# One store per batch of units in place of four, put ahead of a load; the second batch norm's turns moved up, with units and matmuls on zeros about them

## The chip, the cores and the metric

The kernel runs on one core of one Trainium2 chip, as one program with one launch. The metric is the device time in microseconds of that core, from one execution to the next; three runs of the kernel before are shown. One further execution was profiled, and all rows below are from it. TensorE is called PE, VectorE DVE, ScalarE ACT, GpSimd POOL and SyncE SP. SP does nothing here but issue DMA transfers, one after the other, each behind the waits that stand ahead of it.

## The reference

Four graph layers over 512 nodes with 512 features each are run one after the other; ahead of each stands a layer norm and a relu, and behind each a residual sum. Cut to what matters here:

```python
h = relu(layernorm(x)); x = x + L0(h)      # attention with an adjacency mask, feed-forward
h = relu(layernorm(x)); x = x + L1(h)      # linear + prelu, then two convolutions
#   for l in range(2):
#       h = prelu((x + agg(x)) @ conv_W1[l].T + b1[l]) @ conv_W2[l].T + b2[l]
#       h = (h - mean) * rsqrt(var + eps) * gamma[l] + beta[l]     # batch norm over the nodes
#       x = relu(h)
h = relu(layernorm(x)); x = x + L2(h)      # normalised aggregation, then a product with W
h = relu(layernorm(x)); x = x + L3(h)      # two gated relational layers
#   w[r] = sum over 30 bases b of att[r, b] * basis[b]             # 2 x 512 x 512 from 30 x 512 x 512
```

The weights `w` of the two relational layers of L3 depend on no activation. They are sums over 30 bases of 512 x 512 floats, so some 63 MB have to be read for the two layers.

## The kernel before, in words

Node features are kept as [128 partitions, 4 tiles, 512]. Products in float32 precision are made of three matmuls on rounded parts (`_hi`, `_lo`), 128 x 512 each. Every engine runs its own list of instructions in the order in which the code writes them; semaphores tie the lists together. Nothing is reordered.

**Units.** The sum over the bases is cut into 64 units (32 for each relational layer). Unit `u` needs one load of 128 partitions x 2048 floats (1 MB) from `in_basis` into `bring[:, u % 4]`, and four matmuls of 120 rows into 32 columns (`units`, L1241 to L1259), which add into one PSUM bank for each batch of four units. The units are written between the stages of the other layers, so PE has work while they wait for others. When the four units of batch `b` are done, ACT copies the bank into `stage[:, b % 3]` (`stage_units`, L453 to L463; 128 partitions x 512 floats), and SP stores that to `w_scratch` in DRAM. POOL later loads `w_scratch` of a layer as a whole.

**SP's order** (L300 to L319). For `n` from 0, SP issues the load of unit `n` once unit `n - 4` is done (`basis_used`). After the loads with `n % 4 == 3`, from `n = 11` on, it waits until batch `n // 4 - 2` is staged and issues its store, as four transfers of 32 partitions each, since the rows of the four column tiles `j` lie 32 units apart in `w_scratch`. So the load of unit `n + 1` stands behind the store.

**The end of the second batch norm** (PE, L1547 to L1569). PE does the second product of convolution 1 (`c2_1`), then `units(4)` (units 53 to 56), then turns the four normalised tiles `s1` back into node order with 16 transposes (L1554 to L1560), for which it waits tile by tile on `bn1`, then `units(3)` (57 to 59), then the first quarter of the aggregation of the next layer (`aggregate`, L1294 to L1318), unit 60, the other three quarters, unit 61, and the product `gcn`. On ACT the last two batch norm pieces (L605) are followed by the copy of batch 13 (L462), the root of the degrees (L656), and the roots, relus and casts of the layer norm (L419, L662, L665). DVE adds the turned tiles to `xr` (L1118), makes the statistics, and the low parts `x_lo` (L1132), of which the aggregation needs one more for each quarter.

**Matmuls on zeros.** `keep_clock(n)` (L1347 to L1350) does `n` matmuls on a tile of zeros into PSUM bank 7, 128 x 512 in bf16. Before, it is used only at the very beginning.

Of the kernel before, what the change touches and what calls it, by code (L numbers as in the profile page):

```python
# [28 lines left out]
P = 128  # L29
# [39 lines left out]
RELS = 2  # L69
KB = C * BASES  # L70
Q = RELS * C
COLT = 4
UNITS = P // COLT
BATCH = 4
BATCHES = UNITS // BATCH
SLOTS = 3
# [39 lines left out]
def build(nc, x, src, dst, etype, weights, rows, cols, alphas, att, basis, scratch, out):  # L116
    with ExitStack() as ctx:
# [5 lines left out]
        def sem(name):  # L123
            if name not in names:
                names[name] = ctx.enter_context(nc.semaphore(name))
            return names[name]

        bank = [ctx.enter_context(nc.psum_tensor(f"bank{i}", [P, N], F32)) for i in range(4)]
# [3 lines left out]
        def places(*uses):  # L132

            made = []
            for use in uses[:-1]:
# [20 lines left out]
        gate_rows = hT  # L156
# [14 lines left out]
        stage, attw, _, landing, y1_hi, y1_lo = places(  # L171
            [("stage", [P, SLOTS, D], F32), ("attw", [P, 2, BATCH, 32], F32),
             ("unused2", [P, D - 2 * BATCH * 32], F32), ("landing", [P, C, D], F32)],
            [("y1_hi", [P, C, D], F32R), ("y1_lo", [P, C, D], F32R)])
# [34 lines left out]
        zeros = sb("zeros", [P, N], BF16)  # L209
# [23 lines left out]

        def stored(slot, groups):

            return sum(b % SLOTS == slot for b in range(groups)) * COLT * 16

        def weight_parts(name):
            if PARTS[name][0] is None:
# [42 lines left out]
        with nc.Block() as block:  # L282

            @block.sync
            def _(sp):
# [7 lines left out]
                for layer in range(2):  # L293
                    for c in range(C):
                        for r in range(RELS):
                            q = r * C + c
                            sp.dma_start(attw[c * BASES:(c + 1) * BASES, layer, 0, q:q + 1],
                                         att[layer, r, :].rearrange("(b a) -> b a", a=1)).then_inc(
                                             sem("att_loaded"), 16)
                for n in range(2 * UNITS + 2 * BATCH):  # L300
                    if n < 2 * UNITS:
                        if n >= BATCH:
                            sp.wait_ge(sem("basis_used"), n - BATCH + 1)
                        rows = P if n + 1 < 2 * UNITS else KB
                        sp.dma_start(bring[0:rows, n % BATCH, :, :],
                                     basis_rows[n * KB:n * KB + rows, :, :]).then_inc(
                                         sem(f"basis{n % BATCH}_loaded"), 16)
                    if n % BATCH == BATCH - 1 and n >= 3 * BATCH - 1:

                        b = n // BATCH - 2  # L310
                        sp.wait_ge(sem("stage_ready"), b + 1)
                        layer, g = divmod(b, BATCHES)
                        if b == 2 * BATCHES - 1:
                            sp.wait_ge(sem("gate_rows"), 16 * 2 * RELS)
                        for j in range(COLT):
                            at = j * UNITS + g * BATCH
                            sp.dma_start(scratch[layer, at:at + BATCH, :, :].rearrange("g q o -> (g q) o"),
                                         stage[32 * j:32 * j + 32, b % SLOTS, :]).then_inc(
                                             sem(f"w_stored{b % SLOTS}"), 16)  # L319
                for c in range(C):  # L320
                    sp.wait_ge(sem("rel1_out_sum"), c + 1)
                    sp.dma_start(out[:, c, :], hr[:, c, :]).then_inc(sem("out_stored"), 16)
# [904 lines left out]
            def _(pe):  # L1227
# [116 lines left out]
                    mm.then_inc(sem("qkv"[which] + "_psum"), 1)  # L1344

                first, every = FIRST_TILE, TILE_EVERY
                def keep_clock(n):  # L1347

                    for _ in range(n):
                        pe.matmul(bank[7][:, :], zeros[:, 0:P], zeros[:, :], start=True, stop=True)  # L1350

                pe.wait_ge(sem("zeros"), 1)
                keep_clock(12)
# [4 lines left out]
                for n in range(ECH):  # L1358
# [3 lines left out]
                    t, at = divmod(n - first, every)  # L1362
# [128 lines left out]
                for c in range(C):  # L1491
                    for k in range(2 * C):
# [4 lines left out]
                        for i, j in ((0, 0), (0, 1), (1, 0)):  # L1497
                            mm = pe.matmul(bank[c][:, :], (ff1_hi, ff1_lo)[i][k // C][:, k % C, blk(P, c)],  # L1498
                                           weight_parts("f2a" if k < C else "f2b")[j][:, k % C, :],
                                           start=(k == 0 and i == j), stop=(k == 2 * C - 1 and i == 1))  # L1500
# [47 lines left out]
                parts_stage("c1_1", hT_parts, "agg1", "c1_1_psum")  # L1548
                units(1)
                parts_stage("c2_1", x_parts, "c1_1", "c2_1_psum")  # L1550
                units(4)

                pe.wait_ge(sem("c2_1"), C)
                for f in range(C):  # L1554

                    pe.wait_ge(sem("bn1"), f + 1)
                    for c in range(C):
                        mm = pe.transpose(bank[c][:, blk(P, f)], s1[:, f, blk(P, c)], ident[:, :])
                        if f == C - 1:
                            mm.then_inc(sem("x4_psum"), 1)  # L1560
                units(3)

                pe.wait_ge(sem("x5"), 2)
                aggregate("h_gcn_parts", "agg2_psum", order=ALL_BANKS[:C], banks=AGG2_BANKS)
# [132 lines left out]
```

## Time and profile before

| | |
|---|---|
| three runs of the kernel before | 463.43, 464.56, 468.84 us (median 464.56) |
| profiled execution, its own time | 463.99 us |
| its span, first to last instruction | 462.2 us |
| PE busy | 442.4 us (96% of the span) |
| DVE busy | 340.3 us (74%) |
| ACT busy | 241.0 us (52%) |
| POOL busy | 38.4 us (8%) |
| basis loads | 64, of which 63 of 1024 KB and one of 960 KB |
| stores of `stage` | 64 of 64 KB |
| bytes moved by DMA | 99.23 MB, 215 GB/s over the span |

The span is 1.8 us shorter than the execution's own time. A page or a view of the trace gives times in microseconds from the start of the span. Units show as `x8` for one unit, since a float32 matmul is recorded as two. The lines L1256, L1270 and so on are those of the kernel before; those behind L300 have moved by one in the changed kernel.

### The profile page before, as it was taken

What the parts mean: (1) busy time and instruction counts of PE and PEld (TensorE: products, weight loads), DVE (VectorE), ACT (ScalarE), POOL (GpSimd) and SP (SyncE); (2) the same over time, 40 slices, a digit from 0 to 9 for tenths busy, and PEclk for the clock granted to TensorE, in tenths of its full rate; (3) what the DMA queues carried; (4) which work ended last, traced back from release to release, by engine and by line L of the source; (5) the groups of instructions that cost most, each with busy time, mean ns of one, the idle gap of its engine ahead of it and who ended that gap; (6) DMA issues with size and microseconds to landing.
All of it is one profiled execution on the core that took longest, in us unless ns stands there. A gap on an engine that the chain in (4) does not pass through costs nothing.

```text
span 462.2 us, 6176 instructions
## 1 busy us (share of the span) xinstructions
PE 442.4 (96%) x2202; PEld 273.4 (59%) x2202; DVE 340.3 (74%) x725; ACT 241.0 (52%) x421; POOL 38.4 (8%) x59
## 2 busy tenths in 40 slices
PE   5999999899899999999999999999599999999996
PEld 3434434344343334878776866676267688888885
DVE  3897876899999969879779657675758785866212
ACT  3998784586798634663335436445542533511210
POOL 3330000012311200010010000100000000000000
PEclk8899999999999999999999999999889999999999
DMA  7997535123999999856099766772990740000002
GB/s 261 417 365 170 198 116 211 61 92 142 357 397 403 379 386 384 328 164 246 0 358 423 292 238 255 279 251 71 401 340 26 296 150 34 1 0 2 0 3 91
DMA packets 18906, 99.23 MB, mean 215 GB/s; under 512 B 3903, under 2 KB 4287, under 8 KB 8383
## 3 DMA queue, kind: packets, MB, share of 16 engines
q1 hardware_dynamic: 14151, 72.86, 42.2%
q0 software_dynamic: 4000, 25.18, 14.8%
q10 hardware_dynamic: 720, 0.73, 0.5%
q8 instruction: 22, 0.36, 0.3%
q14 instruction: 13, 0.11, 0.1%
HBM read 93.50 MB, written 5.25 MB: 214 GB/s over the span
## 4 chain that ended last, share of the span: by engine, by line
PE 82%; DMA 10%; DVE 6%; issue 1%; ACT 1%; DVEq 0%; SPq 0%; ACTq 0%
PE bank L1270 18%; PE sbank L1592 9%; DMA bring<-in_basis 9%; PE sbank L1256 8%; PE bank L1343 7%; PE sbank L1326 6%; PE bank L1605 6%; PE bank L1498 5%; PE bank L1577 5%; PE bank L1256 3%; PE bank L1310 3%; PE sbank L1236 3%; PE sbank L1310 3%; PE sbank L1381 2%; PE bank L1404 2%; PE sbank L1458 2%
## 5 line engine op out<-in xcount | busy, mean ns | idle before, releaser
L1256 PE MATMUL sbank<-bring,attw 120*32 120x512 f32 x320 | 40.3, 612 | 4.9 <-DMA bring<-in_basis 4.9
L762 DVE TENSOR_SCALAR cnt<-iota_row,edge_f 128x512 bf16<-128x512 f16 x132 | 40.8, 345 | 4.4 <-PE sbank L1326 4.4
L509 ACT ACTIVATE adjT<-distance,edge_w,edge_f 128x128 bf16<-128x128 bf16 x61 | 29.2, 480 | 2.0 <-PE sbank L1326 2.0
L1326 PE MATMUL sbank<-cnt,adjT 128*128 128x512 bf16 x132 | 30.0, 380 | 0.0
L419 ACT ACTIVATE stat<-stat,eps 128x1 f32<-128x1 f32 x32 | 9.4, 295 | 39.0 <-DVE stat L772 39.0
L1343 PE MATMUL bank<-hT,wring 128*128 128x512 f32 x64 | 28.9, 594 | 0.0
L1185 DVE SCALAR_TENSOR_TENSOR y_lo<-sbank,gate,y_hi 128x512 fp32r<-128x512 f32 x16 | 11.8, 749 | 22.6 <-ACT y_hi L690 22.6
L448 ACT ACTIVATE s<-bank,colsb 128x512 f32<-128x512 f32 x24 | 16.4, 687 | 21.8 <-PE bank L1270 21.8
L1256 PE MATMUL bank<-bring,attw 120*32 120x512 f32 x192 | 23.7, 600 | 2.6 <-DMA bring<-in_basis 2.5
L759 DVE TENSOR_SCALAR adjT<-iota_row,edge_f,edge_w 128x128 bf16<-128x128 f16 x71 | 22.1, 311 | 5.4 <-PE sbank L1326 5.4
L480 ACT ACTIVATE distance<-iota_row,edge_f 128x128 bf16<-128x128 f16 x61 | 24.3, 400 | 1.7
L1270 PE MATMUL bank<-hT_hi,w_hi 128*128 128x512 f32 x64 | 25.2, 393 | 0.0
L1270 PE MATMUL bank<-hT_hi,w_lo 128*128 128x512 f32 x64 | 25.0, 390 | 0.0
L1270 PE MATMUL bank<-hT_lo,w_hi 128*128 128x512 f32 x64 | 24.9, 389 | 0.0
L1592 PE MATMUL sbank<-w_hi,xT_hi 128*128 128x512 f32 x64 | 24.9, 389 | 0.0
L1592 PE MATMUL sbank<-w_lo,xT_hi 128*128 128x512 f32 x64 | 24.9, 389 | 0.0
L1592 PE MATMUL sbank<-w_hi,xT_lo 128*128 128x512 f32 x64 | 24.9, 389 | 0.0
L1326 PEld LDWEIGHTS sbank<-cnt,adjT 128*128 128x128 bf16 x132 | 12.3, 98 | 20.5 <-issue 3.6
L1256 PEld LDWEIGHTS sbank<-bring,attw 120*32 120x32 f32 x320 | 8.0, 110 | 26.2 <-issue 19.2
L690 ACT ACTIVATE y_hi<-sbank,gate 128x512 fp32r<-128x512 f32 x16 | 10.8, 688 | 23.8 <-PE sbank L1592 23.8
L531 ACT ACTIVATE s<-s 128x1024 f32<-128x1024 f32 x16 | 16.8, 1058 | 12.2 <-DVE s L947 11.7
L381 POOL TENSOR_TENSOR s<-s,row_sum 128x768 f32<-128x768 f32 x7 | 12.8, 1823 | 94.7 <-ACT row_sum L541 94.7
(227 smaller groups left out, 1062.8 us busy)
## 6 DMA issues: line engine op xcount, KB each, us to landing
bring<-in_basis SPq DMA_DIRECT2D x63, 1024.0 KB, 8.2
wring<-in_weights POOLq DMA_DIRECT2D x8, 1024.0 KB, 10.0
landing<-in_weights POOLq DMA_DIRECT2D x4, 1024.0 KB, 7.2
w_scratch<-stage SPq DMA_DIRECT2D x64, 64.0 KB, 8.0
hT<-in_weights POOLq DMA_DIRECT2D x4, 1024.0 KB, 10.4
qkw<-w_scratch POOLq DMA_DIRECT2D x2, 2048.0 KB, 8.1
rring<-in_rows POOLq DMA_DIRECT2D x12, 256.0 KB, 8.6
hT<-w_scratch POOLq DMA_DIRECT2D x4, 256.0 KB, 6.9
```

The lines of the kernel that those rows point to most:

```text
L480: act.activation(distance[:, i % 2, :], iota[:, 0:P], ACT.Abs, scale=-1.0, bias=dst_lo[:, n:n + 1]).then_inc(sem("distance"), 1)
L509: act.activation(hot_d[:, n % HOT, :], distance[:, i % 2, :], ACT.Relu, scale=minus_w[:, n:n + 1], bias=weight_f[:, n:n + 1]).then_inc(sem ...
L762: dve.tensor_scalar(hot_s[:, n % HOT, :], iota[:, :], src_f[:, n:n + 1], None, ALU.is_equal).then_inc(sem("hot_ready"), 1)
L1256: mm = pe.matmul(unit_bank(b)[32 * j:32 * j + 32, :], attw[0:KB, u // UNITS, g, :], bring[0:KB, u % BATCH, j, :], start=(g == 0), stop=(g ...
L1270: mm = pe.matmul(bank[c][:, :], lhs[:, k, blk(P, c)], rhs[:, k, :], start=(k == 0 and i == j), stop=(k == C - 1 and i == 1))
L1310: mm = pe.matmul(bank[banks[c]][:, :], x[:, k, blk(P, c)].bitcast(dt), counts[:, k, :], start=(k == 0 and i == 0), stop=(k == C - 1 and i ...
L1326: pe.matmul(bank[7][:, :], hot_d[:, n % HOT, :], hot_s[:, n % HOT, :], start=(n == 0), stop=(n == ECH - 1)).then_inc(sem("hot_used"), 1)
L1343: mm = pe.matmul(bank[at][:, :], a, b, start=(k == 0), stop=(k == C - 1))
L1498: mm = pe.matmul(bank[c][:, :], (ff1_hi, ff1_lo)[i][k // C][:, k % C, blk(P, c)], weight_parts("f2a" if k < C else "f2b")[j][:, k % C, :], ...
L1577: mm = pe.matmul(bank[c][:, :], (xT_hi, xT_lo)[i][:, k, blk(P, c)], (root_hi, root_lo)[j][:, k, :], start=(k == 0 and i == j), stop=False)
L1592: mm = pe.matmul(bank[C + c][:, :], (xT_hi, xT_lo)[i][:, k, blk(P, c)], (w_hi, w_lo)[j][:, rel * C + k, :], start=(k == 0 and i == j), sto ...
L1605: mm = pe.matmul(bank[c][:, :], counts[:, k, blk(P, c)], y[:, k, :].bitcast(dt), start=False, stop=(rel == RELS - 1 and k == C - 1 and i = ...
```

## The change

It has two parts. On SP, each batch is stored by one transfer of 4 x 32 x 512 floats in place of four of 32 x 512, with 16 in place of 64 added to its semaphore, and that transfer (with its wait for the staged batch) stands ahead of the load of the same `n`, not behind it. On PE, two of the four units ahead of the turns go behind them, in all four units follow, then two matmuls on zeros, unit 59, three matmuls on zeros, and the aggregation. The zeros go to PSUM bank 4.

```diff
             def stored(slot, groups):
-            return sum(b % SLOTS == slot for b in range(groups)) * COLT * 16
+            return sum(b % SLOTS == slot for b in range(groups)) * 16
...
                 for n in range(2 * UNITS + 2 * BATCH):
+                    if n % BATCH == BATCH - 1 and n >= 3 * BATCH - 1:
+
+                        b = n // BATCH - 2
+                        sp.wait_ge(sem("stage_ready"), b + 1)
+                        layer, g = divmod(b, BATCHES)
+                        if b == 2 * BATCHES - 1:
+                            sp.wait_ge(sem("gate_rows"), 16 * 2 * RELS)
+                        sp.dma_start(scratch[layer].rearrange("(j u) q o -> j u q o", j=COLT)[
+                            :, g * BATCH:(g + 1) * BATCH, :, :].rearrange("j g q o -> j (g q) o"),
+                            stage[:, b % SLOTS, :]).then_inc(
+                                sem(f"w_stored{b % SLOTS}"), 16)
                     if n < 2 * UNITS:
...
-                    if n % BATCH == BATCH - 1 and n >= 3 * BATCH - 1:
...
-                        for j in range(COLT):
-                            at = j * UNITS + g * BATCH
-                            sp.dma_start(scratch[layer, at:at + BATCH, :, :].rearrange("g q o -> (g q) o"),
-                                         stage[32 * j:32 * j + 32, b % SLOTS, :]).then_inc(
-                                             sem(f"w_stored{b % SLOTS}"), 16)
...
-                def keep_clock(n):
+                def keep_clock(n, to=bank[7]):
 
                     for _ in range(n):
-                        pe.matmul(bank[7][:, :], zeros[:, 0:P], zeros[:, :], start=True, stop=True)
+                        pe.matmul(to[:, :], zeros[:, 0:P], zeros[:, :], start=True, stop=True)
...
                 parts_stage("c2_1", x_parts, "c1_1", "c2_1_psum")
-                units(4)
+                units(2)
...
-                units(3)
+                units(4)
+                keep_clock(2, bank[4])
+                units(1)
+                keep_clock(3, bank[4])
 
                 pe.wait_ge(sem("x5"), 2)
```

PE's list from the end of the product `c2_1` (L1270, L1269 in the change) to the first quarter of the aggregation (L1310, L1309), before the change. `bring` are units, four matmuls to a unit; `ident,s` are the turns; `zeros` are the matmuls on zeros. The rows behind the branch are one of its two sides.

```order
L1270 MATMUL bank<-root_lo,w_hi 128x512
L1256 MATMUL sbank<-bring,attw 32x512 x16
L1558 MATMUL bank<-ident,s 128x128 x16
L1256 MATMUL sbank<-bring,attw 32x512 x12
L1315 COMPARE_AND_BRANCH
L1310 MATMUL bank<-adjT,root_hi 128x512
```

The same piece in the changed kernel:

```order
L1269 MATMUL bank<-root_lo,w_hi 128x512
L1255 MATMUL sbank<-bring,attw 32x512 x8
L1557 MATMUL bank<-ident,s 128x128 x16
L1255 MATMUL sbank<-bring,attw 32x512 x16
L1349 MATMUL sbank<-zeros 128x512 x2
L1255 MATMUL sbank<-bring,attw 32x512 x4
L1349 MATMUL sbank<-zeros 128x512 x3
L1314 COMPARE_AND_BRANCH
L1309 MATMUL bank<-adjT,root_hi 128x512
```

Two units (55 and 56) moved from ahead of the turns to behind them, and five matmuls on zeros came in about unit 59.

SP's list at its end, before the change, with the semaphores that a transfer waits for. Two rows make one store of a batch: batch 12, then the loads of units 60 to 62 and of unit 63, then batches 13, 14 and 15 (of the last the first of its four transfers is shown).

```order
L317 DMA w_scratch<-stage 32x512 [waits stage_ready]
L317 DMA w_scratch<-stage 32x512 x3
L305 DMA bring<-in_basis 128x2048 [waits basis_used] x3
L305 DMA bring<-in_basis 120x2048 [waits basis_used]
L317 DMA w_scratch<-stage 32x512 [waits stage_ready]
L317 DMA w_scratch<-stage 32x512 x3
L317 DMA w_scratch<-stage 32x512 [waits stage_ready]
L317 DMA w_scratch<-stage 32x512 x3
L317 DMA w_scratch<-stage 32x512 [waits gate_rows,stage_ready]
```

The same piece in the changed kernel:

```order
L308 DMA w_scratch<-stage 4x32x512 [waits stage_ready]
L316 DMA bring<-in_basis 128x2048 [waits basis_used] x4
L308 DMA w_scratch<-stage 4x32x512 [waits stage_ready]
L316 DMA bring<-in_basis 120x2048 [waits basis_used]
L308 DMA w_scratch<-stage 4x32x512 [waits stage_ready]
L308 DMA w_scratch<-stage 4x32x512 [waits gate_rows,stage_ready]
```

The store of batch 12 now stands ahead of the load of unit 59, the first of the four loads that follow it, and the store of batch 13 ahead of that of unit 63. The same holds for every batch: each store moved up past one load and became one transfer.

## Rows read from the trace of the kernel before

**Rows 1.** The page's chain that ended last: share of the span by engine

```profile
PE 82%; DMA 10%; DVE 6%; issue 1%; ACT 1%; DVEq 0%; SPq 0%; ACTq 0%
```

**Rows 2.** PE's waits over the span: us in total, times, longest us

```profile
PE sbank L1256 <- DMA bring<-in_basis: 4.9, 3, 2.8
PE bank L1256 <- DMA bring<-in_basis: 2.5, 4, 1.4
```

**Rows 3.** PE in order of time, 318 to 346: start, us, what, idle before

```profile
320.09 3.64 PE L1256 MATMUL sbank<-bring,attw 120*32 120x512 f32 x32
323.66 1.97 PE L1558 MATMUL bank<-ident,s 128*128 128x128 f32 x16
326.14 1.06 PE L1256 MATMUL sbank<-bring,attw 120*32 120x512 f32 x8 [0.51 <-DMA bring<-in_basis]
328.85 1.07 PE L1256 MATMUL sbank<-bring,attw 120*32 120x512 f32 x8 [1.65 <-DMA bring<-in_basis]
332.67 1.94 PE L1256 MATMUL sbank<-bring,attw 120*32 120x512 f32 x8 [2.75 <-DMA bring<-in_basis]
```

**Rows 4.** The chain in order of time, 318 to 347: start, us, what

```profile
322.94 9.69 DMA bring<-in_basis
...
339.40 1.12 PE bank L1310 x4
...
341.44 0.91 PE bank L1310 x4
```

**Rows 5.** Stretches: length, busy us of PE, PEld, DVE, ACT, POOL, clock, DMA share, GB/s

```profile
325.60:331.60 6.00, 2.16 (x17) 0.31 (x16) 5.72 (x17) 2.58 (x6) 0.00 (x0) 1.00 0.97 377
331.70:338.40 6.70, 5.73 (x20) 2.84 (x24) 5.28 (x15) 4.29 (x8) 0.54 (x1) 0.50 1.02 431
...
98.00:163.00 65.00, 61.57 (x406) 25.09 (x408) 62.89 (x70) 49.60 (x60) 14.95 (x11) 1.00 0.83 323
182.00:320.00 138.00, 137.96 (x700) 101.47 (x696) 103.94 (x211) 65.07 (x119) 7.48 (x14) 1.00 0.66 248
```

**Rows 6.** ACT in order of time, 296 to 328

```profile
297.66 0.59 ACT L462 COPY stage<-sbank 128x512 f32<-128x512 f32 x1
...
322.07 1.64 ACT L605 ACTIVATE s<-s,stat 128x512 f32<-128x512 f32 x2
```

**Rows 7.** DVE in order of time, 324 to 338

```profile
325.34 0.69 DVE L1118 TENSOR_TENSOR xr<-xr,bank 128x512 f32<-128x512 f32 x1 [2.48 <-PE bank L1558]
...
336.54 0.69 DVE L1132 TENSOR_TENSOR root_lo<-hr,root_hi 128x512 fp32r<-128x512 f32 x1 [0.68 <-ACT root_hi L665]
```

**Rows 8.** SP in order of time, 323.3 to 325.6: the store of batch 12

```profile
323.31 1.90 SPq L317 DMA_DIRECT2D w_scratch<-stage  x4
```

**Rows 9.** The first of these four transfers (L317, 323.4 to 323.6): issue to landing

```profile
DMA to landing us min/median/max: 8.3/8.3/8.3
```

**Rows 10.** SP's DMA queue, 318 to 350: packets, MB, share of 16 engines' time

```profile
q1 hardware_dynamic: 1575, 8.06, 69.9%
```

**Rows 11.** The same queue, 453 to 462.2: the four output stores alone

```profile
q1 hardware_dynamic: 576, 1.05, 30.2%
```

**Rows 12.** The chain in order of time, 9 to 16: two matmuls on zeros

```profile
14.74 0.43 PE sbank L1350 x2
```

**Rows 13.** SP in order of time, 105 to 119.4: loads 13 and 14; batch 1's store

```profile
110.02 1.19 SPq L305 DMA_DIRECT2D bring<-in_basis  x2
...
117.33 1.98 SPq L317 DMA_DIRECT2D w_scratch<-stage  x4
```

**Rows 14.** PE in order of time, 115 to 182.5: units 16, 29, and 32 with 33

```profile
126.90 1.06 PE L1256 MATMUL bank<-bring,attw 120*32 120x512 f32 x8 [1.35 <-DMA bring<-in_basis]
...
167.82 1.07 PE L1256 MATMUL bank<-bring,attw 120*32 120x512 f32 x8 [0.35 <-DMA bring<-in_basis]
...
180.43 1.92 PE L1256 MATMUL sbank<-bring,attw 120*32 120x512 f32 x16
```

**Rows 15.** The load of unit 33, issued at 168.95 (L305): issue to landing

```profile
DMA to landing us min/median/max: 11.3/11.3/11.3
```

More of the change, by code:

```diff
@@ L307, in _ @@
                                          sem(f"basis{n % BATCH}_loaded"), 16)
-                    if n % BATCH == BATCH - 1 and n >= 3 * BATCH - 1:
[L310 to L314, printed above, removed]
-                        for j in range(COLT):
-                            at = j * UNITS + g * BATCH
-                            sp.dma_start(scratch[layer, at:at + BATCH, :, :].rearrange("g q o -> (g q) o"),
-                                         stage[32 * j:32 * j + 32, b % SLOTS, :]).then_inc(
-                                             sem(f"w_stored{b % SLOTS}"), 16)
                 for c in range(C):
```

## Prediction, made before the changed kernel was run

> **What bounds the kernel now.** I read the chain that ended last first, then who waited for whom on PE, then PE and SP in order of time around the changed place. PE has 82% of the chain, DMA 10% [rows 1]. PE is the bound, so an edit gains only where PE waits, where its clock is low, or where another engine is late for it. PE's waits for basis loads are 4.9 us in three (banks 4 to 7) and 2.5 us in four (banks 0 to 3) [rows 2]. The three stand together after the second batch norm: units 57, 58 and 59 wait 0.51, 1.65 and 2.75 us [rows 3]. (A unit is four matmuls, shown as x8, of one 1 MB load; units are counted from 0.) The chain runs through the load of unit 59: issued at 322.94, landed 9.69 us later [rows 4]. In 325.6 to 331.6 PE is busy 2.16 of 6.00 us with the DMA engines at 0.97; before it the granted clock is 1.00 (2.4 GHz), and in 331.7 to 338.4 it is 0.50 (1.2 GHz) [rows 5]. What is costly there is two things: the wait itself and the half clock behind it.
>
> In the attention stretch, 98 to 163, DVE is busy 62.89 of 65.00 us; PE's four waits there are short gaps beside a saturated DVE. In 182 to 320 PE is busy 137.96 of 138.00 us, so no load is late there [rows 5].
>
> **The changed place, step by step.** Now: units 53 to 56 end, PE turns the four tiles at 323.66 in 1.97 us, DVE takes the first result at 325.34. The normalised tiles were ready before: the last two ACT pieces take 1.64 us from 322.07, so they end at 322.9 and 323.7 [rows 3, 6, 7]. After: units 53 and 54 end at about 322.0 (0.86 us each: 320.09 plus two, of four units in 3.64). Tiles 0 and 1 are turned at once (0.5 us each, a quarter of 1.97), tile 2 at 322.95, tile 3 at 323.75, done at 324.25. DVE starts 1.3 us earlier. ACT's copy of a unit batch (0.59 us, L462 [rows 6]), which stands ahead of the square roots in its queue, now waits for unit 55 at 325.15 and ends at 325.75, so the first root, which DVE's statistics allow at about 325.7, comes at 326.0: some 1.0 us of the DVE lead is left.
>
> That lead buys nothing by itself. PE went from unit 59 straight into the first part of the aggregation, and the last operand of the second part was ready at 337.2 (the last L1132, 336.54 plus 0.69), before that part began at 339.4 [rows 4, 7]. The loads decide.
>
> A load goes out when the unit four before it is done. Load 57 goes at 321.2 and 58 at 322.1 as now. Load 59 needs unit 55, which stands behind the turns: 325.2 instead of 322.94, 2.3 us later. Load 60 needs unit 56: 326.05. This delay is hidden, because the DMA queue is backed up: load 58 lands only at 328.8 (PE takes it at 328.85) [rows 3, 4]. Units 55 and 56 run at 324.3 to 326.0, 57 at 326.15, 58 at 328.85 to 329.9, then two matmuls on zeros to 330.3. These cost nothing: PE waits for load 59 there.
>
> **The store.** Four transfers of 32 rows become one of 4 x 32 rows, and it goes ahead of load 59, not behind it. On SP it saves three issues of 0.47 us (four took 1.90) [rows 8], worth nothing where the queue is backed up. What counts is its weight on the DMA engines. The output stores show one 2 KB packet at 0.087 us: 30.2% of 16 engines over 9.2 us is 44.5 us, over the 512 packets of four such stores [rows 11]. The store has 128 such packets. Over 16 engines that is 8 each, 0.7 us; over four engines 32 each, 2.8 us on these four. Each load needs all engines, so the slowest share counts in full. No row shows a 4 x 32 transfer. The nearest row is the one DMA here whose outermost size isn't a multiple of 16, load 63 with 120 rows: in 318 to 350 queue 1 has 1575 packets, of which 6 x 128 + 120 + 12 x 32 = 1272 are data; the other 303 are 18 x 16 + 15, one completion per engine used. So 120 rows went over 15 engines [rows 10]: the number divides the outermost size, which is 4 on the new destination. I take four engines. The Trainium skill ("DMA: Bandwidth & Descriptors", section "Why a DMA increments its semaphore by 16 and not by 1") says that a transfer uses the largest number up to 16 that divides both sides' outermost sizes, which here is 4; by this rule the trace's 15 and my choice agree, and the other end (16) would be wrong.
>
> Load 59 then lands when these four have done 58, the store and 59. On the slowest engine that is 328.8 + 2.8 + 2.5 = 334.1 (2.5 us being 128 packets of 8 KB: the spacing of 326.1 to 328.8 at most). But most engines are ahead of the slowest: the first of today's stores, queued behind load 59, had its 16 completions at 331.6 (323.31 + 8.3), 1.0 us before load 59 was complete [rows 4, 8, 9]. If the four are among them, 333.1. I take 333.5, 0.8 us later than the 332.67 of unit 59 now. With 16 engines: 332.0 to 332.7.
>
> **The clock and the sum there.** At full clock: unit 59 0.86 us, three zeros 0.64 (0.43 for two), eight aggregation matmuls 1.82 (four in 0.91), unit 60 0.86: 4.2 us [rows 3, 4, 12]. Now PE did little in the 7 us before unit 59 and the clock fell. After it does units 57, 58 and two zeros (2.5 us) in 7.3 us and then idles 3.2 us in one piece against 2.75 now. I see no more work in it than before, so I take the fall again. The half clock costs what it costs now: from 332.67 to 338.5 5.8 us at half, 2.9 us lost. The second aggregation then starts at 333.5 + 4.2 + 2.9 = 340.6, against 339.4 now: **+1.2 us**. All behind it is PE's or follows PE without other slack (the loads of units 60 and 61 have 2.5 us and more in hand, and the store of batch 13 goes behind load 62), so this passes to the end. With the clock kept it is 333.5 + 4.2 = 337.7, **-1.7**; with 16 engines too, 332.4 + 4.2 = 336.6, **-2.8**. The zeros' 0.64 us (1.28 at half clock) is on the path in each case.
>
> **The store elsewhere.** Store 1 leaves before load 15 at about 111.3 (load 14 is issued as the second of the pair from 110.02) instead of 117.33, into a queue with little in it, and load 16 no longer stands behind four stores: 117.9 instead of 119.3 [rows 13]. So the wait of unit 16 (1.35 us [rows 14]) shrinks to nothing; DVE, which has no gap for it, keeps the pace: 0, at best -0.6. Against that each later batch puts 2.8 - 0.7 = 2.1 us more on four engines. In the backed-up stretch up to unit 33 four batches do so (stores 2 to 5). Unit 29 waits 0.35 us now [rows 14]. Load 33 lands at 168.95 + 11.3 = 180.2 and unit 33 starts at 181.3 (the second of the pair from 180.43), 1.1 us in hand [rows 14, 15]. The engines' lead, the earlier start and the completions saved take most: 0 to +1.0 us. I take both together as 0. In 182 to 320 the loads stand well ahead of their units. Stores wait for batches that ACT copied long before (batch 12 at 297.66 [rows 6]), so nothing queues behind that wait.
>
> **Sum:** +1.2 us on the profiled execution's own 463.99 gives **465.2 us**. The median of the runs shown, 464.56, is 0.6 above it, the lowest 0.6 below, so I add no correction.
>
> **Rivals.**
> - *Clock kept, four engines.* The zeros and unit 58 do it: -1.7, 462.3. For it: the two zeros stand where PE idles. Against: 3.2 us without work follow them.
> - *Store over all 16 engines.* For it: 128 source rows divide by 16. Load 59 lands by 332.7. With the clock kept 463.99 - 2.8 = 461.2; with the clock fallen 332.4 + 4.2 + 2.9 = 339.5, 464.1, no change.
> - *The backlog reaches PE (slower).* The 2.1 us per batch add up in 125 to 182 and units 29 and 33 wait 1 to 3 us, on top of the +1.2: 466.5 to 469. It decides when load 33 is later than 181.3, 1.1 us more than now.
> - *DVE's earlier start pays.* It can only if load 59 lands before 331.5; the queue excludes that.
>
> **Chances.** Forecast (464.5 to 466.5) 0.50; clock kept with four engines 0.12; 16 engines with clock kept 0.13, with clock fallen 0.12; backlog 0.13. The range reaches from the lowest of these cases to most of the last: 461.2 to 468.3; it leaves out about 1.5 in 10, for half of the 461.2 case and the end of the backlog. 2% is 9.3 us, about what a measurement of this kernel can tell from no change; all cases lie within it: same 0.97, slower 0.02, faster 0.01.
>
> **What would show it.** Each step: unit 59 starting at 333.1 to 334.1, load 59 issued at about 325.2; DVE's first L1117 near 324.1; clock 0.50 over some 6.8 us from about then; the second aggregation at 340.6; one store taking over 4.5 us to land when alone (at the end), against 2.5 now. Wrong if the store's packets run on 16 engines, if the clock stays at 1.00 past 330, or if units 29 and 33 wait over 1 us.

## The result and the profile of the changed kernel

The changed kernel takes 478.03 us (median of four runs, 477.26 to 479.18) against 464.78 us (median of four, 463.43 to 468.84) for the kernel before: a ratio of 1.0272 with a 95% interval of 1.0205 to 1.0339. It is 13.3 us slower, and the forecast was 465.2 us (+1.2) with a range from 461.2 to 468.3. The profiled execution is the one of 477.26 us, with a span of 475.5 us against 462.2.

The page of the changed kernel, part 4, the chain that ended last by engine, which answers to [rows 1], with the line of queue 1 from part 3 (packets, MB, share of 16 engines):

```profile
q1 hardware_dynamic: 13191, 72.85, 40.8%
...
PE 75%; DMA 15%; DVE 6%; ACT 2%; issue 1%; SPq 0%; DVEq 0%; ACTq 0%
```

The waits view of the changed kernel for PE (us in total, times, longest), which answers to [rows 2]:

```profile
PE bank L1255 <- DMA bring<-in_basis: 8.9, 6, 2.5
PE sbank L1255 <- DMA bring<-in_basis: 7.2, 3, 2.9
```

The waits for basis loads rose from 7.4 to 16.1 us. The share of DMA in the chain rose from 10 to 15%. PE in order of time around the changed place, which answers to [rows 3] (start, us, what, idle before):

```profile
331.36 1.92 PE L1255 MATMUL sbank<-bring,attw 120*32 120x512 f32 x16
333.21 1.63 PE L1557 MATMUL bank<-ident,s 128*128 128x128 f32 x12
335.02 0.66 PE L1557 MATMUL bank<-ident,s 128*128 128x128 f32 x4 [0.18 <-ACT s L604]
335.61 2.78 PE L1255 MATMUL sbank<-bring,attw 120*32 120x512 f32 x24
340.55 1.87 PE L1255 MATMUL sbank<-bring,attw 120*32 120x512 f32 x8 [2.15 <-DMA bring<-in_basis]
342.75 0.63 PE L1349 MATMUL sbank<-zeros 128*128 128x512 bf16 x1 [0.33 <-issue]
345.59 1.93 PE L1255 MATMUL sbank<-bring,attw 120*32 120x512 f32 x8 [2.20 <-DMA bring<-in_basis]
```

The stretch of units 53 and 54 begins at 331.36, and in the kernel before at 320.09 [rows 3]: 11.3 of the 13.3 us were lost before the place that the prediction worked out. Starts of single units on PE, read from the same view of both traces (a unit inside a group is placed by its count), show where:

| unit | 15 | 19 | 25 | 29 | 30 | 33 | 42 | 43 | 44 | 54 | 58 | 59 | 60 | 63 |
|---|---|---|---|---|---|---|---|---|---|---|---|---|---|---|
| later by, us | -0.1 | 2.0 | 2.5 | 5.9 | 7.4 | 6.9 | 6.8 | 9.9 | 11.3 | 11.3 | 11.7 | 12.9 | 13.4 | 13.4 |

There are three places: the backed-up stretch up to unit 30 (+7.4, of which 0.5 comes back), unit 43 (+4.5 with what stands behind it), and units 57 to 60 (+2.1). In the first, 2.5 us stand at unit 25, 5.9 at unit 29 and 7.4 at unit 30. The first two places repeat the pattern known from the third: a late load, then half clock. PE in order of time in the first and second place:

```profile
137.06 1.07 PE L1255 MATMUL bank<-bring,attw 120*32 120x512 f32 x8 [2.48 <-DMA bring<-in_basis]
...
171.01 1.07 PE L1255 MATMUL bank<-bring,attw 120*32 120x512 f32 x8 [1.78 <-DMA bring<-in_basis]
173.73 1.94 PE L1255 MATMUL bank<-bring,attw 120*32 120x512 f32 x8 [1.66 <-DMA bring<-in_basis]
...
259.10 1.93 PE L1255 MATMUL sbank<-bring,attw 120*32 120x512 f32 x8 [2.85 <-DMA bring<-in_basis]
```

These are units 19, 28, 29 and 43. The stretches view of the changed kernel (length, busy us of PE, PEld, DVE, ACT, POOL, granted clock, DMA share, GB/s) at the three places, then the two stretches of [rows 5]:

```profile
173.40:176.80 3.40, 3.07 (x10) 0.89 (x11) 2.59 (x6) 0.30 (x1) 0.00 (x0) 0.50 0.78 253
258.70:262.20 3.50, 3.10 (x11) 1.25 (x12) 2.11 (x4) 0.59 (x1) 0.00 (x0) 0.51 1.01 419
...
340.70:350.90 10.20, 7.67 (x26) 2.66 (x21) 7.75 (x19) 5.33 (x10) 0.53 (x1) 0.50 1.01 423
98.00:163.00 65.00, 59.05 (x398) 24.17 (x397) 62.71 (x70) 49.67 (x60) 14.96 (x11) 1.00 0.82 309
182.00:320.00 138.00, 134.99 (x700) 95.73 (x698) 103.28 (x201) 63.06 (x116) 8.51 (x16) 0.99 0.67 253
```

Before, half clock stood once between the start (the first 15 us) and the last microsecond (0.50 in 331.7 to 338.4 [rows 5]); now it stands three times there, 17 us in all. In each of the first two places it costs about 1.5 us beside the wait (unit 30 is 1.5 us later than 29, unit 44 1.4 us later than 43).

### The profile page after: what moved, and what is told of

The parts are those of the page before. It is cut to its first block, busy times and chain, and to the rows that moved or that the text cites. A ratio compares the mean times of both kernels' runs of the same rounds, so it can differ in the third digit from the quotient of the medians.

```text
span 475.5 us, 6132 instructions
## 1 busy us (share of the span) xinstructions
PE 447.5 (94%) x2201; PEld 273.7 (58%) x2207; DVE 340.8 (72%) x725; ACT 241.3 (51%) x421; POOL 38.4 (8%) x59
## 3 DMA queue, kind: packets, MB, share of 16 engines
q1 hardware_dynamic: 13191, 72.85, 40.8%
HBM read 93.50 MB, written 5.25 MB: 208 GB/s over the span
## 4 chain that ended last, share of the span: by engine, by line
PE 75%; DMA 15%; DVE 6%; ACT 2%; issue 1%; SPq 0%; DVEq 0%; ACTq 0%
PE bank L1269 15%; DMA bring<-in_basis 14%; PE sbank L1594 9%; PE bank L1342 7%; PE sbank L1255 6%; PE bank L1607 6%; PE sbank L1325 6%; PE bank L1497 5%; PE bank L1579 5%; PE bank L1255 3%; PE bank L1309 3%; PE sbank L1309 2%; PE sbank L1380 2%; PE sbank L1457 2%; PE bank L1403 2%; PE sbank L1235 1%
## 5 line engine op out<-in xcount | busy, mean ns | idle before, releaser
L1255 PE MATMUL sbank<-bring,attw 120*32 120x512 f32 x320 | 42.1, 633 | 7.2 <-DMA bring<-in_basis 7.2
L1255 PE MATMUL bank<-bring,attw 120*32 120x512 f32 x192 | 24.9, 620 | 8.9 <-DMA bring<-in_basis 8.9
L1269 PE MATMUL bank<-hT_hi,w_hi 128*128 128x512 f32 x64 | 25.1, 393 | 0.0
L1269 PE MATMUL bank<-hT_hi,w_lo 128*128 128x512 f32 x64 | 24.9, 390 | 0.0
L1269 PE MATMUL bank<-hT_lo,w_hi 128*128 128x512 f32 x64 | 24.9, 389 | 0.0
```

The costliest lines, as they stand in the source:

```text
L1255: mm = pe.matmul(unit_bank(b)[32 * j:32 * j + 32, :], attw[0:KB, u // UNITS, g, :], bring[0:KB, u % BATCH, j, :], start=(g == 0), stop=(g ...
L1269: mm = pe.matmul(bank[c][:, :], lhs[:, k, blk(P, c)], rhs[:, k, :], start=(k == 0 and i == j), stop=(k == C - 1 and i == 1))
```

## Why a load is late: the engines under the store

**How many engines carry the store.** Queue 1 moved the same 73 MB in 13191 packets in place of 14151. Both kernels store 16 batches of 128 data packets, so the difference, 960, is completions: 64 x 16 = 1024 before, and 1024 - 960 = 64 = 16 x 4 now. So a store runs on four engines, as forecast. By the rule of the Trainium skill ("DMA: Bandwidth & Descriptors", section "Why a DMA increments its semaphore by 16 and not by 1") it should be four, and the trace agrees.

**What that does to a load.** Units 50 and 51 are the plainest place: the two loads go out one after the other into a queue where nothing of POOL's stands, and in the changed kernel the store stands between them. The instruction view of the loads' line (duration ns, first and last start, then us from issue to landing: the smallest is load 50, the largest load 51), in the kernel before:

```profile
L305 SPq DMA_DIRECT2D bring<-in_basis x2: 328/328/328, 271.4 to 272.3; - x2
DMA to landing us min/median/max: 8.1/9.1/10.1
```

and in the changed kernel:

```profile
L316 SPq DMA_DIRECT2D bring<-in_basis x2: 328/411/494, 282.7 to 283.6; - x2
DMA to landing us min/median/max: 8.9/10.9/13.0
```

Before, 51 lands at 282.4, 2.8 us behind 50 (279.5); issue times and landings are added up. Now it lands at 296.6, 5.0 us behind 50 (291.6). The smallest spacing of two loads in a full queue is 2.5 us in both traces (load 50 of the kernel before lands 2.5 us behind load 49, load 32 of the changed kernel 2.5 behind load 31). Over that the store adds 2.5 us. The packet records give 0.084 us for a packet of 2 KB, so its 32 packets on each of the four engines take 2.7 us (between loads 50 and 51 all 128 start from 291.1 to 293.7). Loads 11, 19, 23, 31, 39 and 47 also land 5.0 us behind the load ahead of them. A load needs all sixteen engines and is complete with the last, and none of the seven shows the store caught up by other engines being ahead. Load 59 lands at the same distance, but it can't be put down to the store alone: it lands 5.0 us behind load 58 in the run with PE's part alone too, whose stores run on sixteen engines and whose load 59 goes out 2.3 us later than before.

Per batch the price is smaller, since before the change the load behind the four stores paid for them: from the landing of load 19 to that of load 23 it was 11.9 us and is 13.0 now. PE pays by the single load: unit 19 had nothing in hand before (it started as its load landed) and comes 2.0 us later.

**Why unit 43 pays more.** SP in order of time in the changed kernel, 237 to 261.5 (start, us, what):

```profile
237.08 2.04 SPq L316 DMA_DIRECT2D bring<-in_basis  x3
239.17 0.51 SPq L308 DMA_DIRECT2D w_scratch<-stage  x1
239.74 16.89 SPq L316 DMA_DIRECT2D bring<-in_basis  x4
```

and POOL in order of time in the same stretch:

```profile
242.04 0.53 POOL L352 DMA_DIRECT2D hT<-in_weights  x1
242.56 0.53 POOL L352 DMA_DIRECT2D landing<-in_weights  x1
```

Here two 1 MB loads of POOL's queue run beside SP's. The chain in order of time in the changed kernel passes through load 43:

```profile
239.17 0.51 SPq L308
239.68 0.06 issue
239.74 19.32 DMA bring<-in_basis
```

In the kernel before the same load took 14.1 us from 232.8, and unit 43 (the last of four from 246.65) began at 249.3:

```profile
L305 SPq DMA_DIRECT2D bring<-in_basis x1: 328/328/328, 232.8 to 232.8; - x1
DMA to landing us min/median/max: 14.1/14.1/14.1
```

It landed at 247.0, 2.3 us ahead of its unit. Now the same load takes 19.3 - 14.1 = 5.2 us longer, and 5.2 - 2.3 = 2.9 is the wait that PE shows (2.85).

That is not the store's own 2.5 us twice over. The two queues take turns on an engine, packet by packet, and the packet records of the trace show it: while POOL's packets of 8 KB run, from 249.2 to 255, the four engines start some ten packets of the store a microsecond, one each 0.39 us on an engine, which is 0.08 for the store's 2 KB and 0.31 for 8 KB of POOL's (2.5 us over the 8 packets that a load has on an engine). So the store's packets lie between 248.3 and 256.2, 7.9 us for what takes 2.7 alone. Each small packet lets a large one by. POOL's two loads have 16 packets on an engine; before, 8 of them went in turn with load 43's own 8 (135 of the 256 on all engines had started when it landed, at 247.0), and 8 came behind it; now, on the four, all 16 go ahead. By this an estimate for the load's delay is 2.7 + 8 x 0.31 = 5.2 us on four engines, 1.3 + 2.5 = 3.8 on eight and 8 x 0.39 = 3.1 on sixteen. Measured: 5.2 here and 4.5 in the run with SP's part alone, 4.0 on eight, 2.7 to 3.2 on sixteen (the runs below). The Trainium skill says so of any two queues ("DMA: Bandwidth & Descriptors", section "Queues, rings and completion order": an engine goes round its queues and changes at packet boundaries), and the trace agrees, with the 0.39 us.

Load 27 is the same case: it lands 8.1 us behind load 26, where 3.6 stood before, with 128 packets of POOL's beside it (157.9 to 162.8) that before ran mostly beside load 28.

## The experiments

Two theories stood against each other at first. T1: the store on four engines ahead of a load makes every fourth load late. T2: the changed order on PE (turns, units, zeros) costs it. Later runs ask how the cost goes with the number of engines, with the place, and what the clock is worth. In all runs the whole computation is done.

**The PE part alone** (the kernel before with PE's list of the change).

> Only the change's PE part: turns after two units, four units behind them, two and three matmuls on zeros about unit 59; the stores as before (four each, behind the load). Theory 1 (the one-transfer store runs on four DMA engines and delays the load behind it by 2.5 us or more, and that delay reaches PE): the PE part is worth between -2.9 us (clock kept) and +1.5 us (clock fallen), so 461 to 466 us, and the attention stretch is as before. Rival 2 (the PE order is what costs, since load 59 is issued 2.3 us later): most of the 13 us is here, 470 us or more.

464.94 us, ratio 1.0005 (0.9981 to 1.0029). PE in order of time of this run:

```profile
328.39 1.06 PE L1256 MATMUL sbank<-bring,attw 120*32 120x512 f32 x8 [1.41 <-DMA bring<-in_basis]
329.39 0.61 PE L1350 MATMUL sbank<-zeros 128*128 128x512 bf16 x2
333.42 1.94 PE L1256 MATMUL sbank<-bring,attw 120*32 120x512 f32 x8 [3.43 <-DMA bring<-in_basis]
```

and its stretch from 330.4 to 337.2:

```profile
330.40:337.20 6.80, 3.78 (x13) 1.38 (x14) 5.38 (x15) 4.40 (x8) 0.54 (x1) 0.50 1.02 411
```

Unit 59 comes 0.75 us later; its load goes out 2.3 us later (325.2). The granted clock falls to 0.50 (1.2 GHz) at 330.4, 0.4 us after the two zeros and 3.0 us before unit 59: two zeros don't hold it. T2 falls: the PE part makes no difference that can be measured.

**The SP part alone** (the changed kernel with PE's list of before).

> Only the change's SP part: one transfer of 4 x 32 rows per batch, ahead of the load; PE as before. Theory 1: it carries nearly all of the loss. In the changed kernel's trace the units have fallen 11.3 us behind before the turns are reached, so +11 to +13.5 us, 475 to 478. Rival 2 (PE order): within 2 us of the kernel before.

478.29 us, ratio 1.0277 (1.0223 to 1.0331), the whole loss (0.3 us over the range of theory 1). Queue 1 has 13191 packets again. From here on only the store is in question.

**One store of 4 x 32, behind the load as before.**

```diff
-                        for j in range(COLT):
-                            at = j * UNITS + g * BATCH
-                            sp.dma_start(scratch[layer, at:at + BATCH, :, :].rearrange("g q o -> (g q) o"),
-                                         stage[32 * j:32 * j + 32, b % SLOTS, :]).then_inc(
-                                             sem(f"w_stored{b % SLOTS}"), 16)
+                        sp.dma_start(scratch[layer].rearrange("(j u) q o -> j u q o", j=COLT)[
+                            :, g * BATCH:(g + 1) * BATCH, :, :].rearrange("j g q o -> j (g q) o"),
+                            stage[:, b % SLOTS, :]).then_inc(
+                                sem(f"w_stored{b % SLOTS}"), 16)
```

> One transfer of 4 x 32 rows per batch, but behind the load as before the change; PE as before. Theory 1 (the number of DMA engines): the load of the same n is freed of the store, but the next one takes its weight of 2.5 us instead, so the loss is nearly that of the SP part as a whole: 471 to 478. Rival 3 (the place ahead of the load is what costs, not the transfer's form): it is gone, 463 to 466.

470.06 us, ratio 1.0131 (1.007 to 1.0193). It falls between the two expectations, 0.9 us under that of theory 1: the form alone costs 6 us, and the place ahead of the load some 8 more with this form. The instruction view of loads 23 and 24 of this run (first and last issue, then the landings; the largest is load 23):

```profile
L305 SPq DMA_DIRECT2D bring<-in_basis x2: 328/331/334, 138.5 to 144.6; - x2
DMA to landing us min/median/max: 8.9/9.4/9.9
```

Load 23 lands at 148.4 and load 24 at 153.5, 5.0 us apart before rounding: the load behind the store takes the 2.5 us, whichever it is. Unit 43 keeps 2.1 us in hand, since the store of batch 8 stands behind its load, and all of the loss lies before unit 30.

**Four stores of 32 rows, ahead of the load.** The block of the stores moves as it is.

```diff
+                    if n % BATCH == BATCH - 1 and n >= 3 * BATCH - 1:
+
+                        b = n // BATCH - 2
...
                     if n < 2 * UNITS:
...
-                    if n % BATCH == BATCH - 1 and n >= 3 * BATCH - 1:
-
-                        b = n // BATCH - 2
...
```

> Four transfers of 32 rows as before, but ahead of the load; PE as before. Theory 1: each of them runs on 16 engines, so only their 0.7 to 1 us goes ahead of the load: within 2 us of before, 463 to 467. Rival 3 (the place): most of the loss, 470 or more, since four issues of 0.47 us and 256 KB stand ahead of the load.

465.79 us, ratio 1.0024 (0.9991 to 1.0057). The place alone can't be told from nothing by the times; in the trace it costs 1.8 us at the end: unit 43 waits here too (+1.4), unit 59 comes 2.4 us later.

**The same rows as one block, 16 engines, ahead.** The rows of `basis` are dealt to units in another order on the host, so that a batch's 128 rows of `w_scratch` lie together; the rest is the change.

```diff
-                        sp.dma_start(scratch[layer].rearrange("(j u) q o -> j u q o", j=COLT)[
-                            :, g * BATCH:(g + 1) * BATCH, :, :].rearrange("j g q o -> j (g q) o"),
+                        sp.dma_start(scratch[layer, g * 16:(g + 1) * 16, :, :].rearrange("r q o -> (r q) o"),
                             stage[:, b % SLOTS, :]).then_inc(
...
-        i[k].reshape(BASES, C, COLT, UNITS, D).transpose(3, 1, 0, 2, 4).reshape(UNITS, KB, COLT, D)
+        i[k].reshape(BASES, C, BATCHES, COLT, BATCH, D).transpose(2, 4, 1, 0, 3, 5).reshape(UNITS, KB, COLT, D)
```

> The changed kernel with the rows of w_scratch dealt out otherwise, so that a batch's 128 rows lie together: the store is one transfer of 128 x 512, still ahead of the load; PE as in the change. Theory 1: its outermost size is 128, it runs on 16 engines (16 completions, 8 packets of 2 KB each, 0.7 us), the loss is gone: 459 to 465. Rival 3 (the place) and a rival that one large transfer is slow whatever its engines: 475 or more.

465.62 us, ratio 1.0045 (1.0011 to 1.008). Loads 50 and 51 of this run:

```profile
L315 SPq DMA_DIRECT2D bring<-in_basis x2: 328/402/476, 272.5 to 273.4; - x2
DMA to landing us min/median/max: 8.6/9.7/10.9
```

They land 3.1 us apart, so the store adds 0.6 us in place of 2.5: eight packets on each of 16 engines. Queue 1 has 13383 packets, which is 14151 - 48 x 16. What is left of the 2.7% is 0.45%: the number of engines is the cause. The time is 0.6 us over the range of theory 1, and those of the two other stores on 16 engines ahead of the load (below) are 0.8 and 1.2 us over it. Theory 1 left out load 43, which took 14.1 us before and here

```profile
L315 SPq DMA_DIRECT2D bring<-in_basis x1: 480/480/480, 232.9 to 232.9; - x1
DMA to landing us min/median/max: 17.3/17.3/17.3
```

3.2 us more, beside POOL's two loads, with a store that adds 0.6 elsewhere. Unit 43 waits 0.8 us for it and comes 1.0 us later than before.

**The same with PE's list of before.**

> Rows together, one store of 128 x 512 ahead of the load, but PE as before the change. Theory 1: against the kernel before it saves the other completions and three issues per batch, which PE feels only where it waits for loads: 461 to 464.5. The difference to the run with rows together and the changed PE order is the PE part: -2.9 if its zeros keep the clock at 1.00, +1.5 if not.

465.25 us, ratio 1.003 (0.9996 to 1.0064), 0.4 us from the run before this one: again no difference from PE's part that can be measured, and neither the 2.9 us gained nor the 1.5 lost. Load 43 takes 16.9 us.

**Eight pieces of 16 rows.** This keeps the change's form of several pieces, with eight as the outermost size.

```diff
-                        sp.dma_start(scratch[layer].rearrange("(j u) q o -> j u q o", j=COLT)[
-                            :, g * BATCH:(g + 1) * BATCH, :, :].rearrange("j g q o -> j (g q) o"),
+                        sp.dma_start(scratch[layer].rearrange("(a u) q o -> a u q o", a=8)[
+                            :, g * 2:(g + 1) * 2, :, :].rearrange("a g q o -> a (g q) o"),
```

467.24 us, ratio 1.0062 (1.003 to 1.0093). Queue 1 has 13255 packets (8 completions to a store). Load 43 takes 18.1 us. Loads 50 and 51 of this run land 3.7 us apart, 1.2 us over the 2.5:

```profile
L316 SPq DMA_DIRECT2D bring<-in_basis x2: 328/397/466, 273.1 to 274.1; - x2
DMA to landing us min/median/max: 8.5/9.8/11.2
```

**Sixteen pieces of 8 rows** (`a=16`, one row of `scratch` each).

> The changed kernel with the rows dealt out so that the store is one transfer of 16 pieces of 8 rows, still strided over w_scratch and of three dimensions, ahead of the load; PE as in the change. Theory 1: 16 engines, so as with the rows together, 459 to 465. Rival 4 (a strided transfer of three dimensions costs more in itself, at issue or in the queue, whatever its engines): like the change, 475 to 478.

466.16 us, ratio 1.0032 (0.9997 to 1.0067), like the single block; load 43 takes 17.0 us. So it is not the stride or the third dimension that costs, but the number of engines:

| engines for a store | added to the next load (51) | added to load 43, beside POOL's | ratio to before, store ahead |
|---|---|---|---|
| 4 | 2.5 us | 5.2, 4.5 us | 1.0272, 1.0277 |
| 8 | 1.2 us | 4.0 us | 1.0062 |
| 16 | 0.6 us | 2.7 to 3.2 us | 1.003, 1.0032, 1.0045 |

The second column halves at each step; the last does not, since a delay costs nothing until a unit's margin is used up.

**One block, 16 engines, behind the load, PE before.**

> Rows together, one store of 128 x 512 on 16 engines, but behind the load as before the change; PE as before. Against the kernel before only the number of transfers differs, 16 in place of 64. Theory 1: unit 43 isn't delayed as it was with the store ahead (1 us there), and fewer completions pass the queue, so 0 to -2 us against before: 462 to 464. Rival (the four transfers cost nothing, and the place is indifferent): as with the store ahead, 465.

463.81 us, ratio 0.9985 (0.9954 to 1.0016). One store in place of four, done without the two harms, can't be told from the kernel before, so no gain that can be measured lies in the merging. It saves 768 completion packets and three issues of 0.47 us a batch, and the time shows neither.

**Only batch 8's store behind its load (43)**, the rest as the change.

```diff
-                    if n % BATCH == BATCH - 1 and n >= 3 * BATCH - 1:
+                    if n % BATCH == BATCH - 1 and n >= 3 * BATCH - 1 and n != 43:
...
+                    if n == 43:
+
+                        b = n // BATCH - 2
...
```

> The changed kernel with one store, that of batch 8 (4 x 32 rows), put back behind the load of unit 43; the other 15 as in the change. In the changed kernel's trace the lag goes from 6.8 to 9.9 us at unit 43 and to 11.3 at unit 44, and POOL's two weight loads are issued at the same time. Theory 1b (a store on four engines costs double where POOL's queue takes turns with SP's on the same engines, and it was the place ahead of load 43 that let this reach PE): unit 43 has its 2 us in hand again, the 4.4 us are gone, 473 to 475 us. Rival (the lag at units 43 and 44 comes from elsewhere, such as later weights): 477 to 479.

474.05 us, ratio 1.0185 (1.0122 to 1.0247), against 478.03 for the change; the slowest of its four executions (474.47) is under the fastest of the change's four (477.26). Load 43 of this run, issued at 241.4, then PE in order of time:

```profile
L316 SPq DMA_DIRECT2D bring<-in_basis x1: 328/328/328, 241.4 to 241.4; - x1
DMA to landing us min/median/max: 15.3/15.3/15.3
```

```profile
255.21 3.64 PE L1266 MATMUL sbank<-bring,attw 120*32 120x512 f32 x32
```

Units 40 to 43 run in one piece with no wait, and half clock stays away there. So one store's place was worth 4.0 us in the times, and in the trace of the change a wait of 2.9 us and 1.4 us of half clock behind it.

**Zeros in the gaps of the kernel before.** SP as before; six zeros between units 57 and 58, ten between 58 and 59.

```diff
-                units(3)
+                units(1)
+                keep_clock(6, bank[4])
+                units(1)
+                keep_clock(10, bank[4])
+                units(1)
```

> The kernel before, with six matmuls on zeros between units 57 and 58 and ten between 58 and 59, which fill the waits of 1.65 and 2.75 us; no other edit. If the half clock behind unit 59 comes from PE's idle time there, the granted clock stays at 1.00 (2.4 GHz) and the 2.9 us that half clock cost come back, less what waits elsewhere: 460.5 to 462. If the clock falls all the same or the zeros delay unit 59: 464 or more. The two zeros of the change, which stand in the same place, did not keep it: it fell at 330.4 in the run with the PE part alone.

461.64 us, ratio 0.9944 (0.9918 to 0.997): the fastest kernel of the study, 0.6% under the kernel before. PE in order of time of this run:

```profile
328.69 1.07 PE L1256 MATMUL sbank<-bring,attw 120*32 120x512 f32 x8 [0.50 <-DMA bring<-in_basis]
329.69 1.47 PE L1350 MATMUL sbank<-zeros 128*128 128x512 bf16 x6
331.22 1.07 PE L1256 MATMUL sbank<-bring,attw 120*32 120x512 f32 x8
332.22 2.33 PE L1350 MATMUL sbank<-zeros 128*128 128x512 bf16 x10
335.06 1.06 PE L1256 MATMUL sbank<-bring,attw 120*32 120x512 f32 x8 [0.51 <-DMA bring<-in_basis]
```

and its stretches 325.6 to 331.6 and 331.7 to 338.4, to be laid beside [rows 5]:

```profile
325.60:331.60 6.00, 5.43 (x42) 2.55 (x38) 3.53 (x10) 1.62 (x5) 0.00 (x0) 1.00 0.98 395
331.70:338.40 6.70, 6.07 (x38) 2.62 (x34) 5.85 (x18) 5.38 (x10) 0.54 (x1) 1.00 1.00 410
```

The clock stays at 1.00 (2.4 GHz), and unit 59 takes 1.06 us in place of 1.94. The loads come no sooner. In this profiled run (463.94 us, the slowest of its twelve) unit 59 is 2.4 us later than before, from a wait of its own at unit 29 and half clock behind it (0.50 from 170.3 to 173.7), and unit 60 is on time again: the full clock gives back 2.35 us.

**The block behind the load, with the same zeros.**

> Both: rows together with the store behind the load, and six and ten matmuls on zeros in the gaps. If the two are independent, the sum of both: 458.5 to 461.5 us. If the earlier landing leaves gaps shorter than the zeros (1.3 and 2.1 us), the zeros stand in the way of units 58 and 59 and up to 1 us is lost.

462.11 us, ratio 0.9959 (0.993 to 0.9988). Its clock is 1.00 too and unit 60 comes 2.5 us earlier than before. It is no faster than the zeros alone and over the 458.5 to 461.5 of the sum, so the two don't add up; all the gain that can be measured goes with the zeros.

## The prediction, step by step

- **Four engines for the store: right,** by the packets of queue 1. The sign that the prediction named came too: the last store, alone in its queue, has its four completions 6.3 us behind its issue (over 4.5 was named), the single block on sixteen engines 3.9. **Its weight of 2.8 us on these four: right,** measured 2.5 over the spacing of two loads.
- **"The engines' lead, the earlier start and the completions saved take most: 0 to +1.0 us. I take both together as 0": the step that failed.** It let the store's weight vanish into a lead of other engines, which one store's completions, 1.0 us ahead of one load, had suggested. Each batch in 125 to 182 was worth 2.1 us by the prediction's own figures and four batches came; against them it set the 1.1 us of unit 33, while units 19, 22, 25 and 29 started as their loads landed. Measured: +7.4 us at unit 30 and +6.9 at unit 33. Of this 2.5 stand at unit 25, 3.4 more come by unit 29 from loads 27 to 29 beside POOL's loads, and 1.5 are half clock behind unit 29's wait. The earlier store 1 and the unhindered load 16, the credit in this term, gave 0.2 us at unit 16. The prediction's own sign of being wrong, unit 29 waiting over 1 us, came (1.66); unit 33 did not wait.
- **"In 182 to 320 the loads stand well ahead of their units": wrong for one load,** and the second cause of the miss: +4.5 us where the sum had nothing. PE busy 137.96 of 138.00 us says that no load was late, not by how much each was early. Load 43 had 2.3 us, beside POOL's loads, and the store costs it 5.2 us there.
- **"But most engines are ahead of the slowest ... I take 333.5, 0.8 us later": the same lead, and here it mattered little.** The spacing of loads 58 and 59 is 5.0 us (340.5 and 345.5) against 3.8 before; 5.0 behind 328.8 is 333.9, between the 333.5 taken and the 334.1 with the 2.8 us in full. The whole place cost 2.2 us (from unit 54 to unit 60) for the 1.2 forecast. How much of it is the store's is open: with PE's part alone the spacing is 5.0 as well, with SP's part alone it is 5.0 too. That the clock falls there again was right, but half clock lasts 10.2 us in place of 6.8.
- **"DVE, which has no gap for it, keeps the pace": right as far as it goes, and no shelter.** At 159.9 of the kernel before (the low part of a weight, `w_lo`) DVE is 0.3 us further behind than at 118, with PE's units 2.5 us behind. But the product and the units that follow the attention are PE's own work and take the 2.5 us along, and behind them DVE is late as well: 2.8 us at 169.2, 6.6 at 173.3.
- **The turns moved up are worth nothing: right.** The first addition of a turned tile starts at 335.39 with units 53 and 54 starting at 331.36, 4.0 us behind them against 5.25 before: a lead of 1.2 us where 1.3 was worked out, and the loads decided. **Two zeros don't hold the clock: right.**
- **The rival "backlog reaches PE"** had the mechanism, with a chance of 0.13, and priced at 1 to 3 us what cost 6.9 by unit 33. It looked at units 29 and 33 alone, and added nothing for a load of POOL's beside the store or for half clock behind a wait.
- **The range** could not hold the result: its upper end came from that price, and no case of it had a late load between 182 and 320.

## What to carry to other kernels

Count on how many DMA engines a small transfer runs (its outermost size on both sides decides here) before it goes into a queue ahead of full-width loads: the next load pays its whole share on the fullest engine, 2.5 us for 256 KB on four engines against 0.6 us on sixteen. Where another queue with large packets is busy, count one of its packets for each small one as long as it has any: 5.2 us on four engines here, and 2.7 to 3.2 even on sixteen. To price such a delay, list for every load how long before its use it lands, not whether PE is idle there now. Where PE must wait for loads, enough filler work in the gap can keep its clock, and that was worth more here (0.6%) than any arrangement of the stores.

## What the hardware showed that was not expected

- A store on four engines delays the following load by about its full per-engine time where the queue is full: 5.0 us between loads in place of 2.5, seven times; 3.7 with eight engines, 3.1 with sixteen.
- Beside loads of POOL's queue the same store costs 5.2 us, since each of its 2 KB packets lets one of POOL's 8 KB by on its engine (one start each 0.39 us). The store on sixteen engines costs 2.7 to 3.2 us there, five times its 0.6.
- The clock: with 16 zeros spread over two gaps it stayed at 1.00 while PE waited for loads in pieces of 0.5 us; with two zeros it fell to 0.50, 0.4 us after them. How few would do between two and sixteen wasn't tried.
- A delayed load costs more than its delay: half clock behind the wait added about 1.4 us at units 29 and 43.
